# Layer 3 without loops: x turned in place, a third Wh buffer, Wh copied ahead of the exponentials, statistics combined on GpSimd

## The chip, the cores and the metric

The kernel runs on one core of a Trainium2 chip. The metric is the device time of one launch in microseconds; lower is better. Engines: PE (TensorE), VectorE (DVE in the profile), ScalarE (ACT), GpSimd (POOL) and SyncE (SP), which issues the stores.

## The reference, cut to what matters

Four graph layers, each followed by a residual and a normalization over the last axis. x is (16, 512, 128). The change touches the fourth only (called layer 3):

```python
Wh = jnp.einsum('bnf,fo->bno', h, W)
s1 = Wh @ a1
s2 = Wh @ a2
e = s1[:, :, None] + s2[:, None, :]
e = jnp.where(e >= 0, e, 0.2 * e)
e = jnp.where(adj[None] == 0, -jnp.inf, e)
attention = jax.nn.softmax(e, axis=-1)
x = layernorm(x + jnp.einsum('bij,bjo->bio', attention, Wh), axis=-1)
```

## The kernel before, in words

Everything stays in SBUF: `m.X` holds x of all 16 batches, a batch as four tiles (`NT`) of 128 rows by 128. Layer 3 is a software pipeline over the batches. Each engine has a list of items with a stage, written out by hand; in step s it does item `name:k` for batch s - k. The items, with their lines:

- PE: `x` (L1458) turns the four tiles of x; `w0`, `w1` (L1468) multiply them with the weights, giving Wh and three more columns with s1 and two scalings of s2; `j` (L1477) spreads s2 over rows, `i` (L1484) s1; `q0` to `q3` (L1507, L1508) put mask and row term into PSUM; `a0` to `a3` (L1496) multiply the exponentials with Wh.
- ScalarE: `XR`, `X` (L1322, L1327) copy the turned x out of PSUM, `W0`, `W1` (L1331) copy Wh, `G` (L1344) makes diagonals of the row term, `L0` to `L3` (L1338) a Relu, `E0`, `E1` (L1349) the exponentials, two tiles at a time.
- VectorE: `m0` to `m3` (L1377) masked row maxima, `c0` (L1391) and `c1` (L1396) the row term out of them (four columns each), `e0` to `e3` (L1385) the sum under the exponential, `d0`, `d1` (L1401) reciprocals, `r0` to `r3` (L1409) division and residual, `b` (L142) the statistics of the normalization, `B` (L148) their aggregation to mean and variance.
- GpSimd: `pool_copy` (L1275) copies x of a batch from `m.X` to `Xf`, from which PE turns it; `pool_norm` takes the root (L155, L157) and applies the normalization in four instructions (L183). The copy of step s stands in front of the normalization of batch s - 3.
- SyncE stores the batch.

Buffers of a batch are doubled: `Wh`, `xT`, `pr` (the exponentials), `r` (`rc` in the profile). `W0` of batch b waits until `a3` of batch b - 2 is done; `x` of batch b waits for `W1` of batch b - 1, since they share a PSUM bank; `a0` waits for `E1`; `r0` of batch b waits until batch b - 2 is stored. The steady part runs in a loop of two steps on each engine (`pairs`); the seam to layer 2 is written out (`tail`), and batch 15 has an end of its own. `hold` is a semaphore increment in front of an instruction.

Of the kernel before, what the change touches and what calls it, by code (L numbers as in the profile page):

```python
# [23 lines left out]
ALU = mybir.AluOpType  # L24
# [1124 lines left out]
def layer3(nc, own, m, bank, out, rl1_at, ready):  # L1149
# [36 lines left out]
    const = sem("const")  # L1186
    x_f = sem("x_copied")
    x_ps = sem("x_turned"); x_c = sem("xT_out"); x_hi = sem("xT_high")
# [35 lines left out]
    def in_order(item, items):  # L1224

        def step(s, par, alive, nth):
            for name, st in items:
                if alive[st]:
                    item(name, s - st, (par + st) % 2, nth + (par - st) // 2)

        return step

# [36 lines left out]
    def pool_copy(pool, s, par, first=False):
        pool.wait_ge(x_ps, after(s - 2, 1))  # L1270
        pool.wait_ge(ready["X"], after(s, 4))
        if not first:
            pool.wait_ge(norm.s_x, after(s - 4, 4))
        hold(pool, gate)
        pool.tensor_copy(flat(Xf[par][:]), batch_flat(m.X, s)).then_inc(x_f, 1)  # L1275

    def pool_last_root(pool):
        rstd, aggr = norm.rstd[1], norm.aggr[1]
        pool.wait_ge(norm.s_x, after(LAST - 2, 4))
        for h in range(2):  # L1280
            two = slice(2 * h, 2 * h + 2)
            pool.wait_ge(norm.s_aggr, after(LAST, 4, 2 * h + 2))
# [5 lines left out]
    def pool_norm(pool, b, par, copied):  # L1288
        pool.wait_ge(x_f, after(copied, 1))
        if isinstance(b, int) and b == LAST:  # L1290
            pool_last_root(pool)
            return
        norm.root(pool, b + CREDIT, par)
        if isinstance(b, int) and b == LAST - 1:
            return
        norm.apply(pool, b + CREDIT, par, r[par], lambda k: r[par][:, k])

    def pool_rest(pool):

        def step(s, par, alive, nth):  # L1300
            if alive[0]:
                pool_copy(pool, s, par)
            pool_norm(pool, s - 3, 1 - par, s if alive[0] else B - 1)

        pairs(pool, B, 4, step, first=4)

# [8 lines left out]
    def act_items(act):  # L1315

        def item(name, b, par, nth):
# [10 lines left out]
            elif what == "W":  # L1328
                act.wait_ge(av, after(b - 2, NT))
                act.wait_ge(wh_ps, after(b, 2, k + 1))  # L1330
                act.copy(Wh[par][:, 2 * k:2 * k + 2, FROM],  # L1331
                         half(b, k)[:, 0:2 * (D + 3)].rearrange("p (t d) -> p t d", t=2)).then_inc(wh_c, 1)
            elif what == "L":
                if k == 0:
# [3 lines left out]
                act.activation(rl[par][:, k], s1_bank(b)[:], ACT.Relu, scale=1.0 - SLOPE,  # L1338
                               bias=Wh[par][:, k, S2_REST:S2_REST + 1]).then_inc(relu, 1)
            elif what == "G":  # L1340
# [28 lines left out]
    def dve_items(dve):  # L1369

        def item(name, b, par, nth):
# [8 lines left out]
            elif what == "e":  # L1380
                if k == 0:
# [3 lines left out]
                dve.scalar_tensor_tensor(out=pr[par][:, k], in0=bank[4 + k % 2][:],  # L1385
                                         scalar=Wh[par][:, k, S2_SLOPE:S2_SLOPE + 1], in1=rl[par][:, k],
                                         op0=ALU.add, op1=ALU.add).then_inc(e_s, 1)
            elif name == "c0":
                dve.wait_ge(s_mx, after(b, NT))
                dve.wait_ge(wh_c, after(b, 2))  # L1390
                dve.scalar_tensor_tensor(out=em[par][:, 0], in0=Wh[par][:, :, S1], scalar=SLOPE - 1.0, in1=mx[par][:],  # L1391
                                         op0=ALU.mult, op1=ALU.subtract).then_inc(e_m, 1)
# [53 lines left out]
    def pe_items(pe):  # L1446

        def item(name, b, par, nth):
            what, k = name[0], int(name[1]) if name[-1].isdigit() else 0
            if what == "x":  # L1450
                pe.wait_ge(x_f, after(b, 1))
                if is_batch(b, 0):
# [32 lines left out]
            elif what == "a":  # L1485
# [35 lines left out]
def layers2_3(nc, m, bank, wide, out, L1):  # L1521
# [4 lines left out]
    with ExitStack() as own:  # L1526
# [131 lines left out]
        def _(pool):  # L1658
# [48 lines left out]
        def _(act):
# [13 lines left out]
            def work(name, b, bp, s, alive):  # L1721
# [50 lines left out]
                elif name == "f":  # L1772
# [8 lines left out]
                 "3E0.0 3W0.1 3W1.1 y.14 3E1.0 3XR.2 3G.1 3L0.1 3L1.1 3X.2 3L2.1 y.15", ACT_ORDER, work, item)  # L1781
            pairs(act, B, 4, third.in_order(item, third.act_order), last=B, first=3)
            third.act_last(act, item)

        @block.vector
        def _(dve):
# [14 lines left out]
            def work(name, b, bp, s, alive):  # L1801
# [44 lines left out]
                elif name == "b":  # L1846
# [7 lines left out]
                 "3m0.1 3m1.1 3e2.0 3e3.0 c1.15 c2.15 3m2.1 3m3.1 3c0.1 3c1.1 b.15", DVE_ORDER, work, item)  # L1854
            pairs(dve, B, 3, third.in_order(item, third.dve_order), last=B, first=2)
            third.dve_last(dve, item)

        @block.tensor
        def _(pe):
# [25 lines left out]
            def product(name, b, bp, s, alive):  # L1885
# [82 lines left out]
                elif name == "d":  # L1968
# [6 lines left out]
            item = third.pe_items(pe)  # L1975
            pe.wait_ge(third.const, 3)
# [41 lines left out]
```

## Time and profile before

| | us |
|---|---|
| median of 3 runs | 933.6 (933.47 to 933.91) |
| the profiled execution | 933.39, its span 931.6 |
| layer 3, steps 3 to 14 | 804.81 to 907.97 |
| busy over the span: PE, DVE, ACT, POOL | 864.7, 624.1, 506.6, 404.0 |

Times in rows are microseconds from the start of the span. In an order of time, a row gives start, busy time, engine, line, operation, output and inputs with shapes, and how many instructions are merged; in brackets, how long the engine was idle before and what ended it. "issue" is idle time for which the profile shows no cause. Matmuls overlap, so their busy times add up to more than the engine's time.

### The profile page before, as it was taken

What the parts mean: (1) busy time and instruction counts of PE and PEld (TensorE: products, weight loads), DVE (VectorE), ACT (ScalarE), POOL (GpSimd) and SP (SyncE); (2) the same over time, 40 slices, a digit from 0 to 9 for tenths busy, and PEclk for the clock granted to TensorE, in tenths of its full rate; (3) what the DMA queues carried; (4) which work ended last, traced back from release to release, by engine and by line L of the source; (5) the groups of instructions that cost most, each with busy time, mean ns of one, the idle gap of its engine ahead of it and who ended that gap; (6) DMA issues with size and microseconds to landing.
All of it is one profiled execution on the core that took longest, in us unless ns stands there. A gap on an engine that the chain in (4) does not pass through costs nothing. (4 is left out here: it accounts for less than half of the span.)

```text
span 931.6 us, 20358 instructions
## 1 busy us (share of the span) xinstructions
PE 864.7 (93%) x6039; PEld 619.7 (67%) x6039; DVE 624.1 (67%) x1931; ACT 506.6 (54%) x903; POOL 404.0 (43%) x451
## 2 busy tenths in 40 slices
PE   6999999999999999977679999999999998999996
PEld 4799999999999998843344444444444444777775
DVE  4756645545545556467676887778876652899997
ACT  4332221211211236566457787888877667888884
POOL 4010211211111225300435788887887776456554
PEclk9999999999999999999979999999999999999999
DMA  9100000000010000000133443333433430010111
GB/s 253 35 9 15 13 12 12 24 12 13 23 30 4 13 1 0 0 0 1 34 70 69 87 102 86 68 78 81 99 82 69 87 86 1 13 34 23 34 34 45
DMA packets 34249, 40.82 MB, mean 44 GB/s; under 512 B 6673, under 2 KB 17553, under 8 KB 34193
## 3 DMA queue, kind: packets, MB, share of 16 engines
q1 hardware_dynamic: 32816, 39.87, 17.9%
q8 instruction: 28, 0.46, 0.2%
q10 hardware_dynamic: 1376, 0.27, 0.1%
q14 instruction: 29, 0.23, 0.1%
HBM read 6.43 MB, written 4.19 MB: 11 GB/s over the span
## 5 line engine op out<-in xcount | busy, mean ns | idle before, releaser
L1686 POOL TENSOR_TENSOR half_sum<-prob 128x1024 f32<-128x1024 f32 x64 | 151.4, 2378 | 21.3 <-PE bank L1950 18.4
L1761 ACT ACTIVATE prob<-wide 128x1024 f32<-128x1024 f32 x128 | 124.1, 1022 | 38.4 <-PE wide L1942 38.1
L460 ACT CAST yT<-wide 128x512 fp32r<-128x512 f32 x48 | 28.1, 589 | 190.8 <-PE wide L870 141.9
L1830 DVE CUSTOM_DVE_ANT_0 junk<-wide,mask_ij 128x512 bf16<-128x512 f32 x128 | 82.8, 684 | 51.2 <-PE bank L1922 50.7
L1938 PE MATMUL wide<-qk_st 128*128 128x512 f32 x256 | 84.5, 437 | 4.9 <-ACT prob L1761 3.3
L1830 DVE CUSTOM_DVE_ANT_0 junk<-bank,mask_ij 128x512 bf16<-128x512 f32 x128 | 83.0, 686 | 0.0
L553 POOL TENSOR_TENSOR Xr<-Xf,Xr 128x512 fp32r<-128x512 f32 x16 | 20.4, 1293 | 140.1 <-ACT Xr L455 139.9
L1496 PEld LDWEIGHTS bank<-Wh,pr 128*128 128x128 f32 x512 | 65.2, 191 | 14.0 <-ACT pr L1349 6.5
L1496 PE MATMUL bank<-Wh,pr 128*128 128x129 f32 x512 | 68.5, 278 | 4.8 <-ACT pr L1349 4.2
L59 PE MATMUL bank<-z,L3T_hi 128*128 128x256 f32 x256 | 72.4, 283 | 0.4 <-DVE z L678 0.4
L61 PE MATMUL bank<-z,L3T_lo 128*128 128x256 f32 x256 | 72.3, 283 | 0.0
L60 PE MATMUL bank<-z,L3T_hi 128*128 128x256 f32 x256 | 72.3, 282 | 0.0
L1938 PEld LDWEIGHTS wide<-qk_st 128*128 128x128 f32 x256 | 46.6, 194 | 32.4 <-DVE mx L1830 18.5
L155 POOL TENSOR_SCALAR n_rstd<-n_aggr 128x4 f32<-128x4 f32 x31 | 6.3, 204 | 129.1 <-DVE n_aggr L148 123.7
L1960 PE MATMUL bank<-prob,v 128*32 128x512 f32 x512 | 61.4, 598 | 0.2 <-ACT prob L1761 0.2
L664 DVE TENSOR_TENSOR yT<-wide,yT 128x512 fp32r<-128x512 f32 x48 | 32.9, 686 | 31.8 <-ACT yT L460 31.8
L687 DVE TENSOR_TENSOR zf<-bank,G 128x256 f32<-128x256 f32 x64 | 27.0, 421 | 34.6 <-PE bank L61 33.1
L59 PEld LDWEIGHTS bank<-z,L3T_hi 128*128 128x128 f32 x256 | 48.8, 191 | 2.0 <-DVE z L678 1.2
L60 PEld LDWEIGHTS bank<-z,L3T_hi 128*128 128x128 f32 x256 | 48.8, 191 | 0.4
L1922 PEld LDWEIGHTS wide<-qkT 32*128 32x128 f32 x128 | 12.3, 184 | 55.2 <-ACT prob L1761 29.2
L61 PEld LDWEIGHTS bank<-z,L3T_lo 128*128 128x128 f32 x256 | 48.9, 191 | 0.0
L558 POOL TENSOR_TENSOR Xa<-X,Xa 128x512 fp32r<-128x512 f32 x16 | 20.6, 1293 | 59.8 <-ACT Xa L429 59.8
(302 smaller groups left out, 2392.0 us busy)
## 6 DMA issues: line engine op xcount, KB each, us to landing
qk_st<-qkT SPq DMA_DIRECT2D x192, 128.0 KB, 2.4
out_dram<-rc SPq DMA_DIRECT2D x15, 256.0 KB, 2.3
Xf<-X SPq DMA_DIRECT2D x14, 256.0 KB, 2.3
A<-in_adj_dram SPq DMA_DIRECT2D x4, 256.0 KB, 5.0
qk_st<-neg_row SPq DMA_DIRECT2D x64, 2.0 KB
Xf<-in_x_dram SPq DMA_DIRECT2D x2, 256.0 KB, 7.0
mask_q<-mask_ji SPq DMA_DIRECT2D x16, 32.0 KB, 1.8
w<-in_L_gnn_W_dram SPq DMA_DIRECT2D x2, 128.0 KB, 2.2
```

The costliest lines, as they stand in the source:

```text
L59: pe.matmul(out, stat[0], mov[0], start=start, stop=False)
L60: pe.matmul(out, stat[0], mov[1], start=False, stop=False)
L61: return pe.matmul(out, stat[1], mov[0], start=False, stop=stop)
L460: act.copy(yT[bb][i][0][:], psum_y[i][:]).then_inc(y_hi, 1)
L664: dve.tensor_tensor(yT[bb][i][1][:], psum_y[i][:], yT[bb][i][0][:].bitcast(F32), ALU.subtract).then_inc(y_lo, 1)
L687: dve.tensor_tensor(zf[:, t], psum_h[k % 2][:, 0:GB * D], G[1 - par][:, 1 if k < NT else 0, t], ALU.add).then_inc(h_sb, 1)
L1496: last = pe.matmul(out_bank[h][:, t * (D + 2):t * (D + 2) + D + 1], pr[par][:, j, k * P:k * P + P], Wh[par][:, j, 0:D + 1], start=(j == 0) ...
L1686: pool.tensor_tensor(flat(half_sum[h][:]), flat(prob[bp][h][:, 0:2]), flat(prob[bp][h][:, 2:4]), ALU.add).then_inc(h_sum, 1)
L1761: act.activation(flat(prob[bp][h][:, 2 * half:2 * half + 2]), wide[half][:], ACT.Exp, scale=SCALE).then_inc(t_exp, 1)
L1830: dve.tensor_tensor_reduce(out=junk[h % 2][:], in0=ROWS[h][:], in1=m.mask_ij[:, i], scale=1.0, scalar=3.0 * MASKED, op0=ALU.add, op1=ALU.m ...
L1938: pe.matmul(bank[j][:], k_st[:, k, j * P:j * P + P], q_st[:, k], start=True, stop=True)
L1960: last = pe.matmul(ring["V0"][c, :], v[bp][:, k, c], prob[bp][h][:, k], start=(k == 0), stop=(k == NT - 1), skip_group_check=True)
```

## The change

- `Xf` and `pool_copy` go; `x` turns `m.X[:, b, t]` itself and waits for layer 2's last write of that batch.
- A third `Wh` takes the freed place; `W0` and `W1` of batch b wait for `a3` of batch b - 3.
- ScalarE's order becomes `L3 W0 E0 W1 E1` for `L3 E0 W0 W1 E1`.
- VectorE no longer does `B` for batches 0 to 14. GpSimd combines the two halves of each statistic in eight operations on 128x4 and then takes the power.
- PE, ScalarE, VectorE and GpSimd run layer 3 written out, without a loop. SyncE keeps its loop.

```diff
-    Xf = [over(f"Xc{k}", [P, NT, D]) for k in range(2)]
+    third_of_Wh = over("Wh2", [P, NT, D + 4])
+    at[0] += 2 * NT * D * 4 - NT * (D + 4) * 4
...
-    Wh = [over(f"Wh{k}", [P, NT, D + 4]) for k in range(2)]
+    Wh = [over(f"Wh{k}", [P, NT, D + 4]) for k in range(2)] + [third_of_Wh]
...
-    ACT_ORDER = staged("L3:2 E0:2 W0:1 W1:1 E1:2 XR:0 G:1 L0:1 L1:1 X:0 L2:1")
-    DVE_ORDER = staged("m0:0 m1:0 d0:2 e0:1 e1:1 r0:2 m2:0 e2:1 e3:1 m3:0 r1:2 d1:2 c0:0 c1:0 r2:2 r3:2 b:2 B:2")
+    ACT_ORDER = staged("L3:2 W0:1 E0:2 W1:1 E1:2 XR:0 G:1 L0:1 L1:1 X:0 L2:1")
+    DVE_ORDER = staged("m0:0 m1:0 d0:2 e0:1 e1:1 r0:2 m2:0 e2:1 e3:1 m3:0 r1:2 d1:2 c0:0 c1:0 r2:2 r3:2 b:2")
...
+        def steps(first, last):
+            for s in range(first, last + 1):
+                for name, back in items:
+                    b = s - back
+                    if 0 <= b < B:
+                        item(name, b, b % 2, b // 2)
...
+    def pool_root(pool, b, par):
+        stats, aggr, rstd, w = norm.stats[par], norm.aggr[par], norm.rstd[par], terms[par]
+        means, sums = (stats[:, :, 1], stats[:, :, 4]), (stats[:, :, 2], stats[:, :, 5])
+        pool.wait_ge(norm.s_stats, after(b, 4))
+        pool.wait_ge(norm.s_x, after(b - 2, 4))
+        hold(pool, gate)
+        pool.tensor_tensor(w[:, 0], means[0], means[1], ALU.subtract).then_inc(s_joined, 1)
+        pool.tensor_tensor(w[:, 1], means[0], means[1], ALU.add).then_inc(s_joined, 1)
+        pool.tensor_tensor(w[:, 2], sums[0], sums[1], ALU.add).then_inc(s_joined, 1)
+        pool.wait_ge(s_joined, after(b, JOINED, 1))
+        pool.tensor_tensor(w[:, 3], w[:, 0], w[:, 0], ALU.mult).then_inc(s_joined, 1)
+        pool.wait_ge(s_joined, after(b, JOINED, 3))
+        hold(pool, gate)
+        pool.tensor_scalar(aggr[:, :, 0], w[:, 1], 0.5, 1.0, ALU.mult, ALU.mult).then_inc(s_joined, 1)
+        pool.tensor_scalar(w[:, 2], w[:, 2], 1.0 / D, EPS, ALU.mult, ALU.add).then_inc(s_joined, 1)
+        pool.wait_ge(s_joined, after(b, JOINED, 4))
+        hold(pool, gate)
+        pool.tensor_scalar(w[:, 3], w[:, 3], 0.25, 1.0, ALU.mult, ALU.mult).then_inc(s_joined, 1)
+        pool.wait_ge(s_joined, after(b, JOINED, 7))
+        pool.tensor_tensor(rstd[:], w[:, 2], w[:, 3], ALU.add).then_inc(norm.s_eps, 1)
+        pool.wait_ge(norm.s_eps, after(b, 1))
+        pool.tensor_tensor(rstd[:], rstd[:], m.neg_half[:, 0:NT], ALU.pow).then_inc(norm.s_rstd, 1)
...
-                act.wait_ge(av, after(b - 2, NT))
+                if b >= 3:
+                    act.wait_ge(av, after(b - 3, NT))
...
-                pe.wait_ge(x_f, after(b, 1))
+                pe.wait_ge(ready["X"], after(b, 4))
...
-                    last = pe.transpose(x_bank(b)[:, t * P:t * P + P], Xf[par][:, t], m.ident[:])
+                    last = pe.transpose(x_bank(b)[:, t * P:t * P + P], m.X[:, b, t], m.ident[:])
...
-            pairs(dve, B, 3, third.in_order(item, third.dve_order), last=B, first=2)
+            third.in_order(item, third.dve_order)(2, B)
...
-            pairs(pe, B, 4, third.in_order(item, third.pe_order), first=3)
+            third.in_order(item, third.pe_order)(3, B + 2)
```

## Rows read from the trace of the kernel before

**Rows 1.** Windows, steps 3 to 14: length, busy PE, PEld, DVE, ACT, POOL, clock, DMA, GB/s

```profile
804.80:907.90 103.10, 99.30 (x663) 76.70 (x663) 94.97 (x336) 85.98 (x170) 59.43 (x83) 1.00 0.11 31
```

**Rows 2.** VectorE in order of time, one step

```profile
847.94 0.69 DVE L1377 CUSTOM_DVE_ANT_0 junk<-wide,mask_ij 128x512 bf16<-128x512 f32 x1 [0.47 <-issue]
...
850.56 0.34 DVE L1409 SCALAR_TENSOR_TENSOR rc<-bank,rec,X 128x128 f32<-128x128 f32 x1
...
851.42 1.41 DVE L1385 SCALAR_TENSOR_TENSOR pr<-bank,Wh,rl 128x512 f32<-128x512 f32 x2
...
853.69 0.15 DVE L1391 SCALAR_TENSOR_TENSOR em<-Wh,mx 128x4 f32<-128x4 f32 x1
853.87 0.16 DVE L1396 SCALAR_TENSOR_TENSOR em<-mx,em 128x4 f32<-128x4 f32 x1
...
854.80 0.87 DVE L142 BATCH_NORM_STATS2 n_stats<-rc 128x6 f32<-128x128 f32 x4
855.83 0.38 DVE L148 BATCH_NORM_AGGREGATE n_aggr<-n_stats 128x2 f32<-128x6 f32 x4 [0.16 <-DVE n_stats L142]
856.40 0.69 DVE L1377 CUSTOM_DVE_ANT_0 junk<-wide,mask_ij 128x512 bf16<-128x512 f32 x1 [0.19 <-issue]
```

**Rows 3.** VectorE in order of time, first instruction of steps 3 and 15

```profile
804.81 0.69 DVE L1377 CUSTOM_DVE_ANT_0 junk<-wide,mask_ij 128x512 bf16<-128x512 f32 x1 [0.43 <-issue]
...
907.97 0.69 DVE L1377 CUSTOM_DVE_ANT_0 junk<-wide,mask_ij 128x512 bf16<-128x512 f32 x1 [0.19 <-issue]
```

**Rows 4.** PE in order of time, several steps

```profile
789.79 1.02 PE L1484 MATMUL wide<-xTc,wB 128*128 128x512 f32 x2
790.66 0.60 PE L1458 MATMUL wide<-ident,Xc 128*128 128x128 f32 x4
...
803.62 0.48 PE L1477 MATMUL wide<-xTr,wB 128*128 128x512 f32 x1
...
811.27 1.15 PE L1496 MATMUL bank<-Wh,pr 128*128 128x129 f32 x8 [0.39 <-ACT pr L1349]
...
817.86 1.02 PE L1484 MATMUL wide<-xTc,wB 128*128 128x512 f32 x2
```

**Rows 5.** ScalarE in order of time, Wh copies and second exponential

```profile
852.53 0.66 ACT L1331 COPY Wh<-wide 128x262 f32<-128x262 f32 x2 [0.80 <-PE bank L1496]
853.07 1.07 ACT L1349 ACTIVATE pr<-pr 128x1024 f32<-128x1024 f32 x1
```

**Rows 6.** GpSimd in order of time, the normalization of one batch

```profile
856.43 0.20 POOL L155 TENSOR_SCALAR n_rstd<-n_aggr 128x4 f32<-128x4 f32 x1 [3.24 <-DVE n_aggr L148]
856.71 1.03 POOL L157 TENSOR_TENSOR n_rstd<-n_rstd,neg_half 128x4 f32<-128x4 f32 x1
857.95 1.58 POOL L183 TENSOR_SCALAR rc<-rc,n_aggr,n_rstd 128x128 f32<-128x128 f32 x2 [0.21 <-POOL n_rstd L157]
```

**Rows 7.** VectorE and GpSimd at once, order of time, three places

```profile
793.68 0.24 DVE L1391 SCALAR_TENSOR_TENSOR em<-Wh,mx 128x4 f32<-128x4 f32 x1
...
792.63 1.27 POOL L1692 TENSOR_TENSOR rb<-rb,X 128x512 f32<-128x512 f32 x1 [3.97 <-DVE rb L1843]
...
7.44 0.67 DVE L636 TENSOR_SCALAR L<-A,col 128x512 f32<-128x512 f32 x1 [0.29 <-DMA A<-in_adj_dram]
...
8.29 0.47 DVE L636 TENSOR_SCALAR L<-A,col 128x512 f32<-128x512 f32 x1
...
7.22 0.61 POOL L549 CAST L_hi<-L 128x512 fp32r<-128x512 f32 x1 [5.38 <-DVE L L640]
...
111.83 0.75 DVE L678 TENSOR_TENSOR z<-G,z 128x256 fp32r<-128x256 f32 x2
...
111.19 1.01 POOL L157 TENSOR_TENSOR n_rstd<-n_rstd,neg_half 128x4 f32<-128x4 f32 x1
```

**Rows 8.** GpSimd's apply of batch 13 and VectorE's `r0` of batch 15

```profile
917.93 3.13 POOL L183 TENSOR_SCALAR rc<-rc,n_aggr,n_rstd 128x128 f32<-128x128 f32 x4 [0.21 <-POOL n_rstd L157]
...
923.67 0.61 DVE L1409 SCALAR_TENSOR_TENSOR rc<-bank,rec,X 128x128 f32<-128x128 f32 x2 [1.06 <-DMA out_dram<-rc]
```

More of the change, by code:

```diff
@@ L1179, in layer3 @@
     rec = [over(f"rec3{k}", [P, NT]) for k in range(2)]
+    terms = [over(f"terms3{k}", [P, 4, NT]) for k in range(2)]
     at[0] = 205120
@@ L1186, in layer3 @@
     const = sem("const")
-    x_f = sem("x_copied")
     x_ps = sem("x_turned"); x_c = sem("xT_out"); x_hi = sem("xT_high")
@@ L1199, in layer3 @@
     stored = [sem(f"stored{k}") for k in range(2)]
+    s_joined = sem("halves_joined")
     last_eps, last_rstd, last_x, last_stored = (sem(f"last_{x}") for x in ("eps", "rstd", "applied", "stored"))
@@ L1224, in in_order @@
     def in_order(item, items):
[L1226 to L1231, printed above, removed]
+        def steps(first, last):
[4 more added lines that the diff above has]
+                        item(name, b, b % 2, b // 2)
+        return steps
     third = Memory()
@@ L1261, in pool_constants @@
     def pool_constants(pool):
-        pool.sem_inc(x_f, CREDIT)
         norm.credit_pool(pool)
         norm.credit_apply(pool)
+        pool.sem_inc(s_joined, CREDIT * JOINED)
         pool.wait_ge(*ready["O"])
-        for n, ap in enumerate((onesb[:], Wh[0][:, :, 0:1], Wh[1][:, :, 0:1])):
+        for n, ap in enumerate((onesb[:], *(w[:, :, 0:1] for w in Wh))):
             pool.memset(ap, 1.0).then_inc(const, 1)
[L1269 to L1275, printed above, removed]
     def pool_last_root(pool):
@@ L1281, in pool_last_root @@
             two = slice(2 * h, 2 * h + 2)
-            pool.wait_ge(norm.s_aggr, after(LAST, 4, 2 * h + 2))
+            pool.wait_ge(norm.s_aggr, CREDIT * 4 + 2 * h + 2)
             hold(pool, gate)
@@ L1286, in pool_last_root @@
             pool.tensor_tensor(rstd[:, two], rstd[:, two], m.neg_half[:, 0:2], ALU.pow).then_inc(last_rstd, 1)
-    def pool_norm(pool, b, par, copied):
-        pool.wait_ge(x_f, after(copied, 1))
-        if isinstance(b, int) and b == LAST:
+    def pool_root(pool, b, par):
[20 more added lines that the diff above has]
+        pool.tensor_tensor(rstd[:], rstd[:], m.neg_half[:, 0:NT], ALU.pow).then_inc(norm.s_rstd, 1)
@@ L1291, in pool_norm @@
+    def pool_norm(pool, b, par):
+        if b == LAST:
             pool_last_root(pool)
             return
[L1293 to L1296, printed above, removed]
+        pool_root(pool, b, par)
+        if b < LAST - 1:
+            norm.apply(pool, b + CREDIT, par, r[par], lambda k: r[par][:, k])
     def pool_rest(pool):
[L1300 to L1303, printed above, removed]
@@ L1305, in pool_rest @@
-        pairs(pool, B, 4, step, first=4)
+        for b in range(B):
+            pool_norm(pool, b, b % 2)
     def act_credits(act):
@@ L1328, in item @@
             elif what == "W":
-                act.wait_ge(av, after(b - 2, NT))
+                if b >= 3:
+                    act.wait_ge(av, after(b - 3, NT))
                 act.wait_ge(wh_ps, after(b, 2, k + 1))
-                act.copy(Wh[par][:, 2 * k:2 * k + 2, FROM],
+                act.copy(Wh[b % 3][:, 2 * k:2 * k + 2, FROM],
                          half(b, k)[:, 0:2 * (D + 3)].rearrange("p (t d) -> p t d", t=2)).then_inc(wh_c, 1)
@@ L1338, in item @@
                 act.activation(rl[par][:, k], s1_bank(b)[:], ACT.Relu, scale=1.0 - SLOPE,
-                               bias=Wh[par][:, k, S2_REST:S2_REST + 1]).then_inc(relu, 1)
+                               bias=Wh[b % 3][:, k, S2_REST:S2_REST + 1]).then_inc(relu, 1)
             elif what == "G":
@@ L1390, in item @@
                 dve.wait_ge(wh_c, after(b, 2))
-                dve.scalar_tensor_tensor(out=em[par][:, 0], in0=Wh[par][:, :, S1], scalar=SLOPE - 1.0, in1=mx[par][:],
+                dve.scalar_tensor_tensor(out=em[par][:, 0], in0=Wh[b % 3][:, :, S1], scalar=SLOPE - 1.0, in1=mx[par][:],
                                          op0=ALU.mult, op1=ALU.subtract).then_inc(e_m, 1)
@@ L1414, in item @@
                 norm.statistics(dve, b + CREDIT, par, r[par])
-            elif what == "B":
-                norm.aggregate(dve, b + CREDIT, par)
         return item
@@ L1510, in pe_items @@
         return item
-    third.sync, third.pool_constants, third.pool_copy, third.pool_norm = sync, pool_constants, pool_copy, pool_norm
+    third.sync, third.pool_constants = sync, pool_constants
     third.pool_rest, third.act_credits, third.dve_credits, third.pe_credits = pool_rest, act_credits, dve_credits, pe_credits
@@ L1695, in _ @@
             third.pool_constants(pool)
-            third.pool_copy(pool, 0, 0, first=True)
             tail("g2.12 S0.14 S1.14 S2.14 r.13 S3.14", POOL_ORDER, work, None)
-            third.pool_copy(pool, 1, 1, first=True)
             tail("g2.13 S0.15 S1.15 S2.15 S3.15 r.14 g2.14", POOL_ORDER, work, None)
-            third.pool_copy(pool, 2, 0, first=True)
-            third.pool_copy(pool, 3, 1, first=True)
             tail("r.15 g2.15", POOL_ORDER, work, None)
-            third.pool_norm(pool, 0, 0, 3)
             third.pool_rest(pool)
@@ L1781, in _ @@
                  "3E0.0 3W0.1 3W1.1 y.14 3E1.0 3XR.2 3G.1 3L0.1 3L1.1 3X.2 3L2.1 y.15", ACT_ORDER, work, item)
-            pairs(act, B, 4, third.in_order(item, third.act_order), last=B, first=3)
+            third.in_order(item, third.act_order)(3, B)
             third.act_last(act, item)
@@ L1975, in _ @@
             item = third.pe_items(pe)
-            pe.wait_ge(third.const, 3)
+            pe.wait_ge(third.const, 4)
             tail("v.15 t2.14 D0.13 D1.13 n.15 t3.14 3x.0 d.13 o.13 t0.15 3j.0 V0.14 V1.14 t1.15 3w0.0 V2.14 V3.14 3w1.0 D0.14 D1.14 "
```

5 lines of the change are left out of this document (3 added, 2 removed).

## The prediction, made before the changed kernel was run

> **What bounds the kernel now.** I read the page first, then the windows over layer 3, then each engine's order of time over two steps. Call step s of layer 3 the stretch that begins with the first row-maximum (`m0`) of batch s on VectorE. Steps 3 to 14 run from 804.81 to 907.97, so one takes (907.97 - 804.81) / 12 = 8.597 us [rows 3]. Over this stretch PE is busy 99.30 of 103.10 us, VectorE 94.97, ScalarE 85.98, GpSimd 59.43 [rows 1]. PE's number invites the wrong reading: its matmuls overlap. Its real need is worked out from starts: from `a0` at 811.27 to `i` at 817.86 are 6.59 us without a stall of note, `i` holds it from 789.79 to 790.66, 0.87, and the transposes `x` are busy 0.60, of which the last 0.15 or so can lie under what follows (`i` is busy 1.02 but gives way after 0.87), 0.45 [rows 4]. That is 7.9 of 8.60 us: PE has 0.7 us to spare.
>
> VectorE has nothing to spare. In one step it goes from `m0` at 847.94 to the end of the statistics at 854.80 + 0.87 = 855.67 with no wait in it, 7.73 us; then come 0.16 us until the four aggregations, 0.38 for them, and 0.19 until the next `m0` at 856.40 [rows 2]. That is 8.46; the mean of 8.597 asks 8.73 of the other kind of step, where the loop turns and the last gap is 0.47, the one in front of the 847.94 row. Both gaps are charged to "issue". So layer 3 is bound by VectorE's instruction stream, and the other engines' waits for each other are slack of it.
>
> **The change, part by part.** *Aggregation off VectorE and the loop gone.* The reader should see two terms in the end of a step. The 0.54 us for waiting and aggregating are removed. The gap before `m0` is 0.19 in a plain step and 0.47 where the loop turns; I take both as gone, because `m0`'s waits can then be worked off behind four statistics of 0.87 / 4 = 0.2 us each and not behind four aggregations of 0.1. VectorE's floor is then 7.73 us. From both sides: with the plain gap kept it is 7.92, with all gaps gone 7.73.
>
> *Wh copied before the exponentials, third Wh.* Now `W0` and `W1` wait for PE's `a3` (0.80 us idle at 852.53) and push the exponential `E1` to 853.07, although its inputs were there at 851.42 + 1.41 = 852.83 [rows 2, 5]. The order by hand with the copies first frees `x` of its wait for `W1`, and `E1` can start some 0.25 earlier. Since VectorE bounds the step, this is worth nothing in itself; it is what lets the others follow. How far: `q3` on PE, then `e3` on VectorE, `E1` (1.07), `a0` close a cycle with PE's own order, about 7.9 us by the same starts. So 7.9 is the floor of the step if VectorE falls under it. Behind the copies on ScalarE stand `E0` and `E1`; `W0`'s input is ready before `E0`'s, so nothing is held.
>
> *x turned where it lies.* Sixteen copies of 0.6 us leave GpSimd, and `x` loses a wait. Four of the copies lie in the seam to layer 2, in front of half sums that wait for PE or ScalarE anyway. I cost it at nothing; its cover is VectorE's 0.7 us over PE. An extra memset of 128x4 is nothing too.
>
> *Nine small GpSimd operations.* Before, GpSimd starts its root at 856.43, the power at 856.71, 0.28 later, and the apply at 857.95, that is 2.28 us after the statistics' end at 855.67 [rows 2, 6]. After: the first of the nine starts 0.23 after the statistics; each of 0.2 with a gap of 0.08 where nothing or one wait stands between, 0.21 where a wait and a semaphore increment do (the gap in front of the apply). Starts: 0.23, 0.50, 0.77, 1.04; mean 1.45, 1.72; 2.13; sum 2.41; power 2.69; apply 2.69 + 1.03 + 0.21 = 3.93. GpSimd does 3.93 + 3.13 = 7.1 us of work per step, below 7.7, so it isn't the bound; behind its new wait for the statistics stands only the batch's own apply, and for that only the store. But the apply of every batch starts 1.65 us later after its statistics. First consequence, in the steady state: the store of b must land before `r0` of b+2. The store lands 2.61 after the apply's end (921.06 to 923.67) [rows 8], so at 3.93 + 3.13 + 2.61 = 9.67 after the statistics; `r0` comes one step and 850.56 - 847.94 = 2.6 later, at 10.6 [rows 2]. Hidden, with 0.9 to spare. Second, at the end: `r0` of batch 15 already waits 1.06 us for the store of batch 13 [rows 8], and all that is left hangs on it. This costs the full 1.65.
>
> *A collision.* This is the term that decides. VectorE's `c0` comes 853.69 - 847.94 = 5.75 after `m0`, `c1` 0.18 later [rows 2]; in the new order, where `m0` follows the statistics at once, 5.75 and 5.93 after their end. Both read two tensors from SBUF. Before, the apply is over by 2.28 + 3.13 = 5.4 [rows 2, 6, 8], and `c0` comes at 6.8. Now the apply's four instructions start at 3.93, 4.71, 5.49, 6.27: `c0` meets the third one, 0.26 in. Does that cost? The one `c0` that overlapped GpSimd work took 0.24 instead of 0.15, at the end of the addition on `rb` [rows 7]. A scaling `L<-A,col` begun at 7.44 under a GpSimd cast took 0.67, the next one without it when it began took 0.47: it got on 0.20 after it began, 0.42 into a cast of 0.61 [rows 7]. On the other hand the subtraction at 111.83 under a power that ran to 112.20 wasn't held at all [rows 7]. So GpSimd keeps VectorE out for part of an instruction. Lower bound for an apply of 0.80: none. Upper: as in the addition, until 0.12 before its end (1.15 of 1.27), that is 0.66. I take the cast's share, the nearest shape (one tensor in): 0.42 / 0.61 x 0.80 = 0.55. `c0` is held from 0.26 to 0.55, 0.29 us; `c1` follows at 0.73, before the fourth begins at 0.78, and passes. What is behind `c0` on VectorE is everything: 0.29 a step.
>
> The Trainium skill, "SBUF — State Buffer", section "Who interferes with whom", says that VectorE with two SBUF inputs and a reading GpSimd instruction exclude each other and that the loser is blocked for the whole instruction. The rows agree that there is such a block, but not that it lasts to the end; by the rule `c0` would lose 0.54 and `c1` another 0.6, and the sum would come out near 939 us.
>
> **Sum.** The step becomes 7.73 + 0.29 = 8.02, above the 7.9 of PE.
> - Start: `m0` of step 3 at 804.81 may come when the row product of 803.62 + 0.48 is seen, 804.24: 0.57 gained [rows 3, 4].
> - Twelve steps: 12 x (8.597 - 8.02) = 6.92 gained.
> - Step 15, whose stretch to the statistics has no gap to lose: 0.29 lost.
> - End: 1.65 lost.
>
> Together 5.55 us. The profiled execution took 933.39 us (span 931.6 and 1.8 around it); less 5.55 is 927.8. The median of the three runs is 0.2 above it: 928.0.
>
> **Rivals.** With a stall s per step, the time is 933.6 - (0.57 + 12 x (8.597 - step) - s - 1.65), with step = max(7.9, 7.73 + s).
> - *No hold.* The apply's reads are short, like the power's. Step 7.9, gain 0.57 + 8.36 - 1.65 = 7.3: 926.3. For it: 111.83. Against it: the two holds above.
> - *Both held* (the other side). The apply keeps VectorE out for 0.64 of its pitch of 0.78. `c0` loses 0.38; `c1` arrives 0.04 into the fourth and loses 0.60. s = 0.98, step 8.71: 12 x -0.11 + 0.57 - 0.98 - 1.65 = -3.4, 937.0. The point from which this decides: s = 0.72 is no gain at all; below 0.57 it is faster, above 0.86 slower by more than can be told from no change (0.2%, 1.9 us, about what a measurement of this kernel resolves).
> - *One and a part.* s from 0.57 to 0.86, as when my chain of nine is off by some tenths so that `c0` meets an instruction at its beginning: 931.7 to 935.5.
> - *Straight code has its own stalls.* The gap in front of `m0` at 804.81 was 0.43 though no loop turned there, against 0.19 later at the same place [rows 3, 2]; it was the first pass over that code. If every step now is a first pass, 13 x 0.24 = 3.1 us come back: 931.1. The Trainium skill, "Runtime: NRT & Kernel Launch", section "Instruction fetch mechanics", says the opposite, that straight code is prefetched and branches stall; by that nothing comes back.
> - *Only the order moves.* Had PE been the bound, the copies and the copy of x would be the gain and VectorE's part none. Against it speaks that VectorE's rows have no wait for PE in them; it would give the same 7.9.
>
> **Chances.** My forecast (s 0.1 to 0.57) 0.45; no hold 0.16; straight code stalls 0.09; one and a part 0.16; both held 0.14. Faster by over 0.2%: the first two and most of the third, 0.68; within 0.2%: 0.18; slower: 0.14. The range runs from 925.5, no hold with a step 0.07 shorter than I read out of PE's starts, to 935.5, where one and a part ends; that leaves out both held and a little below. The likeliest case alone spans 926.4 to 931.7.
>
> **What would show it.** On VectorE: no aggregation in the steps, `m0` straight behind the statistics, and `c0` or `c1` longer than 0.15 and 0.16 us or late by some 0.3 in sum; the start of the apply 3.9 us after the statistics; `x` no longer waiting for `Wh` or a copy; a step near 8.0. At the end: `r0` of batch 15 waits about 2.7 us or more for the store. It is wrong if the step is bound by PE at 7.9 with `c0` untouched (faster), if `c1` is held as well or nine operations take over 4.5 us (slower), or if gaps charged to "issue" appear throughout the straight code.

## The result, and the profile after

The changed kernel takes 925.1 us (median of 5 runs, 924.86 to 925.74) against 933.6 for the kernel before (5 runs, 933.39 to 935.22): a ratio of 0.9909, 95% interval 0.9895 to 0.9923. The forecast was 928.0 with a range from 925.5: right in direction, 2.9 us too high, and the time lies 0.4 below the range. The profiled execution took 925.48 us, its span 923.6; that of before 933.39 and 931.6.

The page (span, busy times, and one DMA queue that brings instructions: packets, MB, share):

```profile
 span 923.6 us, 19931 instructions
...
PE 858.8 (93%) x6021; PEld 621.2 (67%) x6039; DVE 618.9 (67%) x1871; ACT 505.7 (55%) x903; POOL 412.9 (45%) x541
...
q8 instruction: 33, 0.54, 0.3%
```

The window over steps 3 to 14, to be read against [rows 1]:

```profile
804.80:898.30 93.50, 92.87 (x649) 77.69 (x661) 90.63 (x288) 84.78 (x167) 66.95 (x155) 1.00 0.12 33
```

VectorE in order of time, one step and its neighbours, then `m0` of steps 3 and 15, the last statistics of batch 13 and `r0` of batch 15:

```profile
804.78 0.69 DVE L1391 CUSTOM_DVE_ANT_0 junk<-wide,mask_ij 128x512 bf16<-128x512 f32 x1 [0.67 <-PE wide L1489]
...
842.80 0.87 DVE L142 BATCH_NORM_STATS2 n_stats<-rc 128x6 f32<-128x128 f32 x4
843.78 0.69 DVE L1391 CUSTOM_DVE_ANT_0 junk<-wide,mask_ij 128x512 bf16<-128x512 f32 x1
...
849.69 0.14 DVE L1405 SCALAR_TENSOR_TENSOR em<-Wh,mx 128x4 f32<-128x4 f32 x1
849.87 0.16 DVE L1410 SCALAR_TENSOR_TENSOR em<-mx,em 128x4 f32<-128x4 f32 x1
849.96 0.61 DVE L1423 SCALAR_TENSOR_TENSOR rc<-bank,rec,X 128x128 f32<-128x128 f32 x2
850.60 0.87 DVE L142 BATCH_NORM_STATS2 n_stats<-rc 128x6 f32<-128x128 f32 x4
851.58 0.69 DVE L1391 CUSTOM_DVE_ANT_0 junk<-wide,mask_ij 128x512 bf16<-128x512 f32 x1
...
898.38 0.69 DVE L1391 CUSTOM_DVE_ANT_0 junk<-wide,mask_ij 128x512 bf16<-128x512 f32 x1
...
905.20 0.88 DVE L142 BATCH_NORM_STATS2 n_stats<-rc 128x6 f32<-128x128 f32 x4
...
915.10 0.61 DVE L1423 SCALAR_TENSOR_TENSOR rc<-bank,rec,X 128x128 f32<-128x128 f32 x2 [2.06 <-DMA out_dram<-rc]
```

A step now takes (898.38 - 804.78) / 12 = 7.80 us; before it took 8.597 [rows 3]. The two spans differ by 8.0 us, and five stretches add up to it:

| stretch | before | after | gained |
|---|---|---|---|
| all before `m0` of step 2 (code not changed up to the seam) | 795.63 | 796.13 | -0.50 |
| step 2 | 9.18 | 8.65 | +0.53 |
| steps 3 to 14 | 103.16 | 93.60 | +9.56 |
| step 15, to the end of batch 13's statistics | 7.72 | 7.70 | +0.02 |
| from there to the end | 15.91 | 17.52 | -1.61 |

The first row can't be laid to the change. The power in layer 2's set-up, far ahead of the changed code, on GpSimd in order of time, in this execution and then in another execution of the same kernel (e12_changed_again):

```profile
440.80 0.54 POOL L1679 TENSOR_TENSOR bn_terms<-bn_terms,neg_half 128x1 f32<-128x1 f32 x1
```

```profile
438.98 0.54 POOL L1679 TENSOR_TENSOR bn_terms<-bn_terms,neg_half 128x1 f32<-128x1 f32 x1
```

Two executions of one kernel lie 1.8 us apart there, more than the 0.50 in question.

GpSimd in order of time, one batch, and ScalarE in order of time in the same step:

```profile
843.89 0.20 POOL L1291 TENSOR_TENSOR terms<-n_stats 128x4 f32<-128x4 f32 x1 [1.60 <-DVE n_stats L142]
844.04 0.20 POOL L1292 TENSOR_TENSOR terms<-n_stats 128x4 f32<-128x4 f32 x1
...
845.70 1.03 POOL L1306 TENSOR_TENSOR n_rstd<-n_rstd,neg_half 128x4 f32<-128x4 f32 x1
846.95 3.13 POOL L183 TENSOR_SCALAR rc<-rc,n_aggr,n_rstd 128x128 f32<-128x128 f32 x4 [0.22 <-POOL n_rstd L1306]
```

```profile
846.82 0.40 ACT L1345 COPY Wh<-wide 128x262 f32<-128x262 f32 x1
847.07 1.10 ACT L1363 ACTIVATE pr<-pr 128x1024 f32<-128x1024 f32 x1
848.03 0.41 ACT L1345 COPY Wh<-wide 128x262 f32<-128x262 f32 x1
848.86 1.06 ACT L1363 ACTIVATE pr<-pr 128x1024 f32<-128x1024 f32 x1 [0.42 <-DVE pr L1399]
```

The statistics end at 842.80 + 0.87 = 843.67, the apply starts at 846.95: 3.28 us later. The apply runs to 850.08, so `c0` at 849.69 and `c1` at 849.87 both lie inside it, and take 0.14 and 0.16 us, as long as without it. Nothing is held here; `c0` comes 2.74 us after the apply began, 0.39 or 0.40 into its fourth instruction (3.13 / 4 = 0.78 each). What sets the step is PE (e7 below tests it), in order of time:

```profile
842.20 1.14 PE L1508 MATMUL bank<-Wh,pr 128*128 128x129 f32 x8
...
848.70 1.02 PE L1496 MATMUL wide<-xTc,wB 128*128 128x512 f32 x2
...
850.00 1.14 PE L1508 MATMUL bank<-Wh,pr 128*128 128x129 f32 x8
```

Between the two `a0` (842.20 and 850.00) lie 7.80 us, and no row between them has a wait.

### The profile page after: what moved, and what is told of

It reads as the page before. It is cut to its first block and busy times, and to the rows that moved or that the text cites. A ratio compares the mean times of both kernels' runs of the same rounds, so it can differ in the third digit from the quotient of the medians.

```text
span 923.6 us, 19931 instructions
## 1 busy us (share of the span) xinstructions
PE 858.8 (93%) x6021; PEld 621.2 (67%) x6039; DVE 618.9 (67%) x1871; ACT 505.7 (55%) x903; POOL 412.9 (45%) x541
## 5 line engine op out<-in xcount | busy, mean ns | idle before, releaser
L1399 DVE SCALAR_TENSOR_TENSOR pr<-bank,Wh,rl 128x512 f32<-128x512 f32 x64 | 46.0, 743 | 3.2 <-PE bank L1520 1.6
```

## The experiments

Medians and ratios to the kernel before, with 95% intervals. A step is again the distance of `m0` to `m0` in layer 3, the one that most of the twelve have. The runs were taken in three groups, each beside the kernel before, so ratios compare better than times: e1 to e4, e5 to e8, e9 to e12.

| run | us | ratio | step, us |
|---|---|---|---|
| e1_loops_only | 930.89 | 0.9964 (0.9952 to 0.9977) | 8.39 |
| e2_loops_stats | 935.73 | 1.0015 (1.0003 to 1.0027) | 8.68 |
| e3_no_wh | 932.18 | 0.9976 (0.9960 to 0.9991) | 8.39 |
| e9_wh_loops | 925.53 | 0.9915 (0.9902 to 0.9928) | 8.02 |
| e4_dve_aggr | 925.59 | 0.9907 (0.9886 to 0.9927) | 7.97 |
| e12_changed_again | 924.34 | 0.9895 (0.9880 to 0.9909) | 7.80 |
| e5_two_casts | 929.26 | 0.9943 (0.9926 to 0.9959) | 8.14 |
| e6_one_add | 930.70 | 0.9956 (0.9939 to 0.9972) | 8.27 |
| e7_no_mask | 924.06 | 0.9882 (0.9866 to 0.9899) | 7.64 |
| e8_tail | 923.89 | 0.9883 (0.9866 to 0.9899) | 7.80 |
| e10_r15 | 923.22 | 0.9897 (0.9879 to 0.9916) | 7.80 |
| e11_both | 922.23 | 0.9877 (0.9863 to 0.9891) | 7.80 |

**Loops only** (kernel before, written out).

```diff
+def straight(eng, steps, depth, step, first=0, last=None):
+    for s in range(first, steps + depth - 1 if last is None else last + 1):
+        step(s, s % 2, [0 <= s - k < steps for k in range(depth)], s // 2)
...
-            pairs(dve, B, 3, third.in_order(item, third.dve_order), last=B, first=2)
+            straight(dve, B, 3, third.in_order(item, third.dve_order), last=B, first=2)
```

> The kernel before with only the loops of layer 3 written out on PE, ScalarE, VectorE and GpSimd; nothing else changed. Theory (VectorE bounds the step, and the loop cost it two things: 0.28 us of extra gap at each turn, 0.14 a step, and about 0.20 a step between c1 and r2, where the wait is against a register in the loop and the gap is 0.29, against 0.09 in the changed kernel): step 8.60 - 0.34 = 8.26, time near 929.5. Rival (the loop costs only its turn): step 8.46, time near 931.9. Rival (straight code stalls for its instructions): no gain, gaps charged to issue.

VectorE in order of time, first `r2` of the kernel before (its `c1` is the 853.87 of [rows 2]), then this run:

```profile
854.15 0.61 DVE L1409 SCALAR_TENSOR_TENSOR rc<-bank,rec,X 128x128 f32<-128x128 f32 x2
```

```profile
854.27 0.16 DVE L1401 SCALAR_TENSOR_TENSOR em<-mx,em 128x4 f32<-128x4 f32 x1
854.36 0.61 DVE L1414 SCALAR_TENSOR_TENSOR rc<-bank,rec,X 128x128 f32<-128x128 f32 x2
...
856.58 0.69 DVE L1382 CUSTOM_DVE_ANT_0 junk<-wide,mask_ij 128x512 bf16<-128x512 f32 x1 [0.18 <-PE wide L1482]
```

From the start of `c1` to that of `r2` it was 0.28 us in the loop and is 0.09 now, so the loop cost more than the gaps in front of `m0`. But the step is 8.39 and not the 8.26 of the expectation, and `m0` now waits for PE. Something else stands at 8.39.

**Without the Wh part** (the changed kernel with the old order and the old wait).

```diff
-    ACT_ORDER = staged("L3:2 W0:1 E0:2 W1:1 E1:2 XR:0 G:1 L0:1 L1:1 X:0 L2:1")
+    ACT_ORDER = staged("L3:2 E0:2 W0:1 W1:1 E1:2 XR:0 G:1 L0:1 L1:1 X:0 L2:1")
...
-                if b >= 3:
-                    act.wait_ge(av, after(b - 3, NT))
+                act.wait_ge(av, after(b - 2, NT))
```

> The changed kernel with the Wh part undone: ScalarE's old order (E0 before W0), and W0 waits for a3 of batch b-2. Theory (PE's order and the hand-over e3, E1, a0 bound the changed kernel, and Wh in front of E1 and of x lengthens that chain by 0.2 to 0.3): step 8.0 to 8.1, time near 928. Rival (VectorE bounds the changed kernel too): step and time as changed, 7.80 and 925.1.

PE and then ScalarE, in order of time:

```profile
857.88 1.05 PE L1507 MATMUL bank<-Wh,pr 128*128 128x129 f32 x8
...
860.63 1.16 PE L1507 MATMUL bank<-Wh,pr 128*128 128x129 f32 x8 [0.24 <-ACT pr L1362]
```

```profile
858.97 0.66 ACT L1344 COPY Wh<-wide 128x262 f32<-128x262 f32 x2 [1.32 <-PE bank L1507]
859.51 1.07 ACT L1362 ACTIVATE pr<-pr 128x1024 f32<-128x1024 f32 x1
```

This is the other thing: `a3` on PE (857.88), the two Wh copies when it is done (858.97), `E1` (859.51), `a0` (860.63), on which PE waits. The previous `a0` came at 852.24, 8.39 earlier, the same step as in e1. The expectation was 8.0 to 8.1. With this chain back, a step is 0.59 longer than in the changed kernel, 7.1 us over twelve; by the ratios (0.9976 against 0.9909) the launch is 6.3 us longer.

**Loops out and statistics on GpSimd** (the copy of x and the old Wh stay: e1 with the `pool_root` of the change and no `B` on VectorE).

> Loops written out and the statistics combined on GpSimd, but x is still copied on GpSimd behind the apply, and Wh is still copied after the first exponential with two buffers. Theory (the copy of x is what would bind): the apply ends 6.4 us after the statistics instead of 5.4, the copy 7.3 after, x 7.4, and from x to the next m0 are 1.95, so a step of about 9.3 and a time near 942, slower than before. Rival (VectorE's own stream decides): step 8.26 - 0.73 = 7.5 to 7.9, time 923 to 926.

GpSimd, VectorE and PE round one copy of x, in order of time:

```profile
854.45 0.87 DVE L147 BATCH_NORM_STATS2 n_stats<-rc 128x6 f32<-128x128 f32 x4
...
861.96 0.61 POOL L1284 COPY Xc<-X 128x512 f32<-128x512 f32 x1 [0.26 <-POOL rc L188]
862.07 0.51 DVE L1428 SCALAR_TENSOR_TENSOR em<-mx,em 128x4 f32<-128x4 f32 x1
862.62 0.66 PE L1490 MATMUL wide<-ident,Xc 128*128 128x128 f32 x4 [0.69 <-POOL Xc L1284]
...
864.67 0.69 DVE L1409 CUSTOM_DVE_ANT_0 junk<-wide,mask_ij 128x512 bf16<-128x512 f32 x1 [0.66 <-PE wide L1509]
```

Slower than before by 0.15%, though not by as much as the 942 expected. The copy stands behind the later apply, PE waits for it, and `m0` for PE. The cycle is real but goes round in two steps, which I had missed: from the statistics' end (855.32) to the copy's 7.25, then 0.05, from `x` to `m0` 2.05, from `m0` to the statistics' end 8.02; 17.37 / 2 = 8.68. So the statistics on GpSimd need x turned in place. `c1` under the copy takes 0.51 for 0.16.

**Loops and Wh alone** (e1 plus the changed order and the third Wh. The third Wh needs the room of `Xf`, so x is turned in place; PE still waits for a GpSimd copy of 480 of the 512 columns to a place that nothing reads).

> Only the loops and the Wh part of the change: aggregation on VectorE, two-operation root, and before every x on PE a GpSimd copy of 480 of the 512 elements of each row that PE waits for, in the old place of GpSimd's queue (into a scratch tile; PE still turns x in place, since there is no room for the copy beside the third Wh). Theory (turning x in place only pays once the apply comes later; two steps hold 6.2 until the copy ends, 2.1 from x to the m0 after, 7.5 to the statistics, 15.8 in sum, so 7.92 a step, under VectorE's 7.42 + 0.54 = 7.96): step 7.97, as with the aggregation on VectorE and no copy; time near 925 to 926. Rival (x in place is worth something in itself): step over 8.1.

0.9915: nearly the whole gain of the change, with the aggregation still on VectorE. The steps alternate between 7.97, which was expected, and 8.06 or 8.07. Three things are together here, though: the order, the third Wh, and turning x where it lies.

**Aggregation back on VectorE** (the changed kernel with `B:2` in the order and the old root).

```diff
-    DVE_ORDER = staged("m0:0 m1:0 d0:2 e0:1 e1:1 r0:2 m2:0 e2:1 e3:1 m3:0 r1:2 d1:2 c0:0 c1:0 r2:2 r3:2 b:2")
+    DVE_ORDER = staged("m0:0 m1:0 d0:2 e0:1 e1:1 r0:2 m2:0 e2:1 e3:1 m3:0 r1:2 d1:2 c0:0 c1:0 r2:2 r3:2 b:2 B:2")
...
-        pool_root(pool, b, par)
+        norm.root(pool, b + CREDIT, par)
```

> The changed kernel with the aggregation back on VectorE and the two-operation root on GpSimd. Theory (VectorE's stream bounds this one again): 0.16 + 0.38 + 0.19 on top of 7.52, step 8.25, apply 1.0 earlier after the statistics at the end of the kernel, time near 929.5. Rival (PE bounds, VectorE has room): step under 8.0, time under 927.

VectorE in order of time, aggregation, `m0` and the next `m0`:

```profile
852.23 0.38 DVE L148 BATCH_NORM_AGGREGATE n_aggr<-n_stats 128x2 f32<-128x6 f32 x4
852.53 0.69 DVE L1391 CUSTOM_DVE_ANT_0 junk<-wide,mask_ij 128x512 bf16<-128x512 f32 x1
...
860.50 0.69 DVE L1391 CUSTOM_DVE_ANT_0 junk<-wide,mask_ij 128x512 bf16<-128x512 f32 x1
```

VectorE bounds this one: no row of the step has a wait, and `e2` and `e3` take 1.40 us together where they take 1.56 in the changed kernel, which has them wait for PE. The expected step was 8.25; the numbers of the rival came (under 8.0, under 927), but not its reason, that PE bounds. Of the 7.97, 0.54 are waiting and aggregating, so VectorE's stream without them is 7.43 us, not 7.73. The statistics on GpSimd gain 12 x 0.17 = 2.0 us in the steps and lose 1.6 at the end (from the end of batch 13's statistics on, 15.91 here and 17.52 in the changed kernel); 0.9907 against 0.9909 and 0.9895 does not tell them apart.

**What holds VectorE.** Two casts, or one addition, of 128x480 put between the third and fourth instruction of the apply, over `c0` and `c1`.

```diff
+                if k == 3:
+                    for n in range(2):
+                        pool.tensor_copy(dump[:, 480 * n:480 * n + 480], batch_flat(m.X, b)[:, 0:480])
```

> The changed kernel with two extra GpSimd casts (128x480, into a scratch tile that nobody reads) between the third and the fourth apply instruction of every batch, where VectorE's c0 and c1 fall. Theory (whether c0 and c1 are held depends on the GpSimd instruction: copy, cast and two-input additions hold VectorE's two-input instructions for most of their length, the apply's scaling by pointers does not): c0 or c1 stretched by some 0.4 us in sum, VectorE's step 7.5 + 0.4, step 7.9 to 8.0, +1 to +3 us. Rival (nothing of the kind exists in the steady state): c0 0.14, c1 0.16, step 7.80, same time.

GpSimd and VectorE in order of time:

```profile
874.46 1.12 POOL L1320 CAST dump<-X 128x480 bf16<-128x480 f32 x2
874.51 0.55 DVE L1413 SCALAR_TENSOR_TENSOR em<-Wh,mx 128x4 f32<-128x4 f32 x1
875.09 0.50 DVE L1418 SCALAR_TENSOR_TENSOR em<-mx,em 128x4 f32<-128x4 f32 x1
```

```diff
+                if k == 3:
+                    pool.tensor_tensor(dump[:], batch_flat(m.X, b)[:, 0:480], batch_flat(m.X, b)[:, 0:480], ALU.add)
```

> The same place, one GpSimd addition of 128x480 with two inputs, about 1.2 us, from 5.6 to 6.8 us after the statistics; c0 falls 0.4 into it. Theory (held to 0.1 before its end): c0 takes 0.14 + 0.7, step 7.5 + 0.7 = 8.2 to 8.3, +5 us. Rival (no hold): c0 0.14, step 7.80, same time.

```profile
869.23 0.99 POOL L1319 TENSOR_TENSOR dump<-X 128x480 f32<-128x480 f32 x1
869.26 0.97 DVE L1412 SCALAR_TENSOR_TENSOR em<-Wh,mx 128x4 f32<-128x4 f32 x1
```

Under the casts `c0` takes 0.41 longer and `c1` 0.34, about twice the 0.4 expected in sum; under the addition `c0` takes 0.83 longer, as expected. Each time VectorE gets on only 0.10 to 0.15 before the GpSimd instruction ends. The holds are real, and go straight into the step: 8.14 - 0.72 = 7.42 and 8.27 - 0.83 = 7.44, the same stream of VectorE as in e4 (with 0.39 and 0.33 as the means over the steps). The apply in the same place holds nothing, but e7 will show that this is a matter of the moment.

**PE 0.2 us each lighter in four places** (the mask products left out).

```diff
-                pe.matmul(bank[4 + k % 2][:], m.identb[:], m.mask_ji[:, k], start=True, stop=False)
-                pe.matmul(bank[4 + k % 2][:], onesb[:], flat(dg[par][:]), start=False, stop=True).then_inc(r_ps, 1)
+                pe.matmul(bank[4 + k % 2][:], onesb[:], flat(dg[par][:]), start=True, stop=True).then_inc(r_ps, 1)
```

> The changed kernel without the mask's four products per batch on PE, so the exponent is left unmasked; 4 x 0.22 = 0.87 us less on PE per step. Theory (PE's unbroken order bounds the changed kernel at 7.80; VectorE's own stream needs 7.52, the 7.69 between m0 and the end of the statistics less the 0.17 that the sums wait for q3): step 7.5 to 7.6, 12 x 0.25 = 3 us faster than the changed kernel, near 922. Rival (VectorE bounds it): step 7.80, same time as the changed kernel. Rival (the hand-over e3, E1, a0 bounds it): between, 7.6 to 7.8.

VectorE, ScalarE and PE round one `E1`, in order of time:

```profile
854.01 1.40 DVE L1399 SCALAR_TENSOR_TENSOR pr<-bank,Wh,rl 128x512 f32<-128x512 f32 x2
855.45 1.06 ACT L1363 ACTIVATE pr<-pr 128x1024 f32<-128x1024 f32 x1 [0.65 <-DVE pr L1399]
856.56 1.16 PE L1508 MATMUL bank<-Wh,pr 128*128 128x129 f32 x8 [0.52 <-ACT pr L1363]
858.17 0.69 DVE L1391 CUSTOM_DVE_ANT_0 junk<-wide,mask_ij 128x512 bf16<-128x512 f32 x1
```

With PE lighter the step falls only to 7.64, not to 7.4: the rival of the expectation, the hand-over. `m0` to the end of `e3` takes 4.88, then 0.04, `E1` 1.06, 0.05, and from `a0` to the next `m0` 1.61; together 7.64. (`m0` before this one came at 850.53; one step of the twelve took 8.10, with a wait of 0.38 for a store.) That the step fell at all shows that PE bounds the changed kernel. The time says less: 0.9882 is not told apart from the 0.9909 and 0.9895 of the changed kernel, whose intervals it overlaps. The changed kernel thus has three limits close together: VectorE 7.42, hand-over 7.64, PE 7.80.

In this run `c0` and `c1` come earlier within the apply, and there they are held. The fourth instruction of the apply with `c0`, or `c0` and `c1`, in two steps:

```profile
848.51 0.80 POOL L183 TENSOR_SCALAR rc<-rc,n_aggr,n_rstd 128x128 f32<-128x128 f32 x1
848.64 0.33 DVE L1405 SCALAR_TENSOR_TENSOR em<-Wh,mx 128x4 f32<-128x4 f32 x1
```

```profile
886.77 0.81 POOL L183 TENSOR_SCALAR rc<-rc,n_aggr,n_rstd 128x128 f32<-128x128 f32 x1
886.84 0.14 DVE L1405 SCALAR_TENSOR_TENSOR em<-Wh,mx 128x4 f32<-128x4 f32 x1
887.02 0.22 DVE L1410 SCALAR_TENSOR_TENSOR em<-mx,em 128x4 f32<-128x4 f32 x1
```

`c0` at 848.64, 0.13 into the instruction, takes 0.33 for 0.14 and is done 0.46 into it; `c1` at 887.02, 0.25 into it, takes 0.22 for 0.16 and is done 0.47 into it; `c0` at 886.84, 0.07 into it, passes. The other steps of this run agree: what begins from 0.12 to 0.25 into the fourth instruction is done at 0.45 to 0.47. So the apply does hold VectorE, until about 0.32 into each instruction of 0.8. In the changed kernel `c0` comes at 0.39 or 0.40 in every step but the first, just behind that. The most that such a hold cost here is 0.19, and 7.42 + 0.19 = 7.61 still lies under PE's 7.80.

**The end.** e8 lets VectorE aggregate batches 13 and 14 again, so that their root takes two operations; e10 puts batch 15's result into `rl[0]`, free by then, so that `r0` does not wait for batch 13's store; e11 does both.

```diff
+                if b >= LAST - 2:
+                    dve.wait_ge(norm.s_stats, after(b, 4))
+                    hold(dve, norm.gate)
+                    for n in range(4):
+                        dve.bn_aggr(norm.aggr[par][:, n], norm.stats[par][:, n]).then_inc(norm.s_aggr, 1)
```

> The changed kernel with batches 13 and 14 aggregated on VectorE and rooted in two operations again. Theory (the end hangs on apply and store of batch 13, which start 3.28 us after its statistics instead of 2.28): r0 of batch 15 waits about 1.1 us instead of 2.06, time 1.0 less than the changed kernel, about 0.989 x before. Rival: VectorE's extra 0.7 us per batch there eats it, no change.

```diff
+    last_r = rl[0][:, 0].rearrange("p (t d) -> p t d", t=NT)
...
-                    dve.wait_ge(stored[par], (nth + 1) * 16)
-                dve.scalar_tensor_tensor(out=r[par][:, k], in0=out_bank[h][:, t * (D + 2) + 1:t * (D + 2) + D + 1],
+                    dve.wait_ge(e_s, after(LAST - 1, NT)) if b == LAST else dve.wait_ge(stored[par], (nth + 1) * 16)
+                dve.scalar_tensor_tensor(out=last_r[:, k] if b == LAST else r[par][:, k], in0=out_bank[h][:, t * (D + 2) + 1:t * (D + 2) + D + 1],
```

> The changed kernel with batch 15's result in a place of its own (a Relu tile that is free by then), so that r0 of batch 15 doesn't wait for the store of batch 13. Theory (the end hangs on that store): the 2.06 us wait is gone; the root of batch 14, on GpSimd until 9.6 us after the statistics of batch 13, then comes ahead of batch 15's root and gives back about 1: 1 us less than the changed kernel. Rival (another chain ends as late): no change.

> The changed kernel with both: batches 13 and 14 aggregated on VectorE and rooted in two operations, and batch 15's result in a place of its own. Theory: 1.0 from the shorter chain and 1.0 from the store that isn't waited for, 2 us less than the changed kernel, near 923. Rival: the two gains are the same microsecond, 924.

> The changed kernel once more, beside the three above on the same chip. Both theories: step 7.80, ratio near 0.991.

e11's apply of batch 13 and `r0` of batch 15, in order of time:

```profile
906.86 3.15 POOL L183 TENSOR_SCALAR rc<-rc,n_aggr,n_rstd 128x128 f32<-128x128 f32 x4 [0.21 <-POOL n_rstd L1319]
...
911.63 0.61 DVE L1432 SCALAR_TENSOR_TENSOR rl<-bank,rec,X 128x128 f32<-128x128 f32 x2
```

From the end of batch 13's statistics to the end of the span: 17.52 us changed (17.53 in e12), 15.92 in e8, 15.42 in e10, 15.01 in e11. In e8 `r0` waits 1.05 us for the store, as expected, and the end is 1.60 shorter where 1.0 was expected; in e10 it is 2.10 shorter (expected 1). In e11 `r0` comes 7.04 after the statistics, with no wait for a store, against 9.02 (915.10 - 906.08) in the changed kernel. e11 is the fastest, 922.23 us. In the trace its edit is worth 2.5; against the changed kernel run beside it (e12, 924.34) the medians differ by 2.1, and the two intervals of the ratio overlap, as they do for e8 and e10.

## Why the prediction was wrong in size

**The collision, the step that failed.** The prediction has "`c0` is held from 0.26 to 0.55, 0.29 us" a step, and so a step of 7.73 + 0.29 = 8.02, bound by VectorE. Measured are a hold of nothing and a step of 7.80, bound by PE. Two parts of the term failed. First the place: the apply starts 3.28 after the statistics and not 3.93. GpSimd's two-input operations follow each other at 0.155 us and not at 0.27 (0.35 of the difference), and the two places with a semaphore increment among the nine took 0.25 and 0.27 instead of 0.41 (the rest). So `c0` falls 0.39 into the last instruction of the apply, not 0.26 into the third. Then the length: the hold under the apply ends about 0.32 into the instruction (e7), not at 0.55. At the predicted place it would have cost 0.06, at the real one it costs nothing. The price was taken from the nearest shape, "one tensor in"; a cast, a copy and an addition hold VectorE to nearly their end (e5, e2, e6), the apply for less than half of its length, and the power of before not at all [rows 7]. That `c0` misses it altogether is luck of some 0.07 us, and the number of the no-hold rival came without its reason, that the apply's reads hold nothing. Taken without the hold, the prediction's own formula gives 12 x 0.12 = 1.4 us less in the steps and nothing lost in step 15, 926.3.

**PE's floor.** "about 7.9" from starts in several places; in one piece, `a0` to `a0`, it is 7.80. From `a0` to `i` it takes 6.50 (842.20 to 848.70), where the stretch read before had 6.59. A tenth over twelve steps is 1.2 us. With both mended, 926.3 - 1.2 = 925.1: that is what was measured, though part of the agreement is chance, as the 0.50 before the change shows. The low end of the range allowed 0.07 for that reading, and so missed by 0.4.

**VectorE's floor.** 7.73 was read off the loop. Straight code runs the same instructions in 7.42 (e4, e5, e6 agree): besides the gap at the turn, the gaps inside went (`c1` to `r2` 0.28 to 0.09). With this floor even the predicted hold would have been covered, 7.42 + 0.29 = 7.71 under PE's 7.80; and without the hold so would 7.73. Only both errors together put VectorE above PE.

**"Worth nothing in itself".** This was the deeper error, hidden because the parts came together. VectorE did bound the kernel before, at 8.60, but the chain `a3`, `W0`/`W1`, `E1`, `a0` stood at 8.39, right below, where the prediction saw only PE at 7.9. The rows were read: 0.80 us of ScalarE waiting for `a3` [rows 5]. They were priced at 0.25 in `E1`'s start, and not followed round to the next `a0`. So the loops alone yield 0.2 a step (e1), the Wh part is worth 0.59 in the changed kernel (e3), and loops with Wh give nearly all (e9). For the rival **only the order moves** this means: PE did not bound before, but once the loops are out the order and the third Wh carry most of the gain. The GpSimd statistics, which carried most of the prediction's text, gain 0.17 a step.

**What held.** Start: 0.57 foreseen, 0.53 measured. End: 1.65 foreseen, 1.61 measured, though by other terms, so that the agreement is luck: the apply is 3.28 - 2.28 = 1.00 later, and so `r0` of batch 15, at 9.02 instead of 7.98; the remaining 0.6 lies behind it, and goes in e8, but no run shows what it is. `r0` waits 2.06 us for the store instead of 1.06; "about 2.7" was expected. Step 15 lost nothing, as nothing was held there. x in place brought no new wait, and e2 shows what it spares once the statistics are on GpSimd; no run has it alone.

**Straight code stalls** did not come about: VectorE has no gap charged to "issue" in steps 3 to 14, although more instructions were brought (33 packets and 0.54 MB on that queue against 28 and 0.46). The Trainium skill, "Runtime: NRT & Kernel Launch", section "Instruction fetch mechanics", says that prefetch is sequential, and that a taken branch stalls when its target is not in the two pages at hand. The traces agree for the straight code; whether the 0.28 us more at the loop's turn are such a stall no run shows. **Both held** and **one and a part** fell with the hold. The Trainium skill's "SBUF — State Buffer", section "Who interferes with whom", has the loser blocked for the whole instruction: e5 and e6 agree for casts and the addition, nearly to the full length, while under the apply of e7 the block ends 0.32 us into an instruction of 0.80.

Left open: why the apply holds for less than half of its length and a cast for nearly all of it. Its 128 columns for 480, its scalars or its operation could be the reason; no run separates them. Nor does a run separate the third Wh from the new order.

## What to carry to other kernels

Before calling an engine the bound, follow every wait of the others round to where it closes, and write the length of each cycle beside the engine's; one that stands 0.2 us below the bound takes most of the gain of an edit that lowers the bound alone. Read an engine's floor from one unbroken stretch, start to start of the same instruction. What an overlap costs must be priced by the same kind of instruction, not by the nearest shape, and at the moment where the other falls into it. A term that decides between two limits is worth only what it lifts one above the other: read both limits first.

## What the runs showed of the hardware

- GpSimd held a VectorE instruction with two SBUF inputs until 0.10 to 0.15 us before its own end when it was a cast (0.56 each, `c0` +0.41), a copy (0.61, `c1` +0.35) or an addition (0.99, `c0` +0.83). Under the apply, a tensor with two scalars per partition (0.8 each), what began 0.12 to 0.25 into an instruction was held until about 0.32 into it (e7, up to +0.19), and what began at 0.39 or later was not held (changed kernel, 0.14 and 0.16).
- GpSimd's two-input operations on 128x4, recorded at 0.20 us, start 0.155 apart; those with one input and two constants start 0.27 apart.
- A loop of two steps cost VectorE (8.60 - 0.54) - 7.43 = 0.63 us a step over the same instructions written out (e4).
- Code ahead of the change ran 1.8 us apart in two executions of one kernel (440.80 and 438.98).
